# A two-layer language-model tower on one core: how the tables that name each tile's expert are packed, read into registers and placed in TensorE's stream

## The chip, the core and the metric

The kernel runs on one core of a Trainium2 chip. The metric is the device time of one execution in microseconds (us): 1137.43 as the median of three runs, which lie between 1136.9 and 1138.49. Beside the timed runs there is one profiled execution, from which all rows below come.

An engine has two parts that matter here. Its **sequencer** takes the instructions in program order; semaphore waits that stand alone, register arithmetic and register loads are carried out there. Products, copies and activations are handed on to a queue in front of the engine proper, so that a sequencer may be ahead of its engine.

## The reference, cut to what matters

Tokens are embedded and normalised, pass a state-space layer, then a first mixture of experts, then an attention layer, then a second mixture of experts. Only the two mixtures are touched:

```python
# first: 8 experts, 2 picked for each of 4000 tokens, hidden width 512
# second: 64 experts (8 groups of 8), 4 picked for each token, hidden width 256
h = jax.nn.relu(xf @ W1e + b1e)
y = h @ W2e + b2e
acc + cwe[:, None] * y
```

Everything is float32, the width of a token is 128.

## The kernel before

The picked (token, expert) pairs are sorted by expert into blocks of 128 rows. Because an expert's last rows and the next expert's first rows can share a block, the work is cut into **tiles**: one tile is one block under one expert. The first mixture has 63 blocks and 70 tiles, the second 126 blocks and 252 tiles. Which block and which expert a tile has is known only at run time: VectorE writes it into two small int32 tables on one partition, `tile_tables` (for each tile the offset of the expert's second weights, and the place of the next tile's block in the ring of turned blocks) and `stage_tables` (the offset of the expert's first weights).

Each engine's loop over tiles is written out flat; the order in the program is the order of the code, and semaphores tie the engines together. For tile u:

- GpSimd (POOL, line 867) gathers the 128 rows of a block from memory, eight blocks ahead at most.
- TensorE (PE) turns a block (`turn`, line 633), makes the first product of tile u+1 (`first`, line 638), waits for the middle layer of tile u (line 674), and makes its second product (`second`, line 645). Each float32 product of 128 by 128 is carried out as two passes; a tile of the first mixture has 8 + 8 passes, of the second 4 + 4, and a turn is one pass.
- VectorE (DVE) copies a turned block out (line 554), makes half of the bias and relu (`rectify`, line 559) and copies the expert's first weights for tile u+3 into a ring (`stage`, line 550). In the second mixture it later also combines results (line 1328). ScalarE makes the other half of the relu (line 605) and copies results out (line 623).

PE and DVE hold the table's words in registers. The class `Words` keeps 16 registers for a round of eight tiles, four words (two tiles) to a load; after each odd tile the four registers just used are loaded anew for the next round:

```python
self.engine.reg_load(self.regs[2 * u:2 * u + 4], self.table[0:1, bass.ds((first_tile + (self.first + u)) * 2, 4)])
...
second(words.value(u, 0), u)
if u % 2 and first_tile + u + RING < c.tiles:
    words.load(first_tile + RING, u - 1)
```

A word is a finished offset, so `value` needs one fused register instruction, which also forms the address. The second product needs one more for each further 128 rows of the weights.

Of the kernel before, what the change touches and what calls it, by code (L numbers as in the profile page):

```python
# [18 lines left out]
I32 = mybir.dt.int32  # L19
I16 = mybir.dt.int16  # L20
U32 = mybir.dt.uint32
ALU = mybir.AluOpType
ACT = mybir.ActivationFunctionType
AX = mybir.AxisListType

D = 128
# [66 lines left out]
SPAN = 16384  # L93
KEEP = {0: 32, 1: 67}


# [61 lines left out]
def tower_kernel(nc, a, out):  # L158
# [15 lines left out]
    with ExitStack() as ctx:  # L174
# [86 lines left out]
        b1r = sb("b1r", [128, 2, 128])  # L261
        table = sb("table", [1, 2 * TAB], I32)
        w0 = 2 * FFN[0].tab
        assert 2 * w0 <= 2 * TAB <= 512
        tile_tables = [table[0:1, 0:w0], cst[0:1, 128:128 + 2 * TAB].bitcast(I32)]
        stage_tables = [table[0:1, w0:2 * w0], table[0:1, 0:2 * TAB]]
        place = [sb("place", [128, 4, NT], I32)] * 2
# [190 lines left out]

        def pairs_of(engine, table, tau, n, top_a, top_b):

            _, words = nc.values_load_multi_w_load_instructions(
                table[0:1, bass.ds(tau * 2, 2 * n)], engines=[engine], min_val=0, max_val=max(top_a, top_b),
                skip_runtime_bounds_check_because="the tables hold clipped numbers of experts and places in the ring")

            def within(word, top):
                return nc.s_assert_within(word, 0, top, skip_runtime_bounds_check_because="the tables hold clipped numbers")
            return [within(w, top_a) for w in words[0::2]], [within(w, top_b) for w in words[1::2]]

        class Words:

            def __init__(self, engine, p, table, first, top_a, top_b):
                self.engine, self.table, self.first, self.tops = engine, table, first, (top_a, top_b)
                self.regs = [engine.alloc_register(f"{p}word{n}") for n in range(2 * RING)]
                for u in range(0, RING, 2):
                    self.load(0, u)

            def load(self, first_tile, u):
                self.engine.reg_load(self.regs[2 * u:2 * u + 4], self.table[0:1, bass.ds((first_tile + (self.first + u)) * 2, 4)])

            def value(self, u, which):  # L480
                word = self.engine.snap(self.regs[2 * u + which], min_val=0, max_val=max(self.tops))
                return nc.s_assert_within(word, 0, self.tops[which], skip_runtime_bounds_check_because="the tables hold clipped numbers")

            def free(self):
                for r in self.regs:
                    self.engine.free_register(r)
# [55 lines left out]
        def expert_vector(dve, c, combine_pick):  # L542
# [22 lines left out]
            dve.wait_ge(S(f"w{c.n}_ld"), 16 * weight_loads(c))  # L565
            w1, _ = pairs_of(mybir.EngineType.DVE, stage_tables[c.n], 0, 2, (c.E - 1) * c.wcols, (KEEP[c.n] - 1) * 128)
            words = Words(dve, p, stage_tables[c.n], 2, (c.E - 1) * c.wcols, (KEEP[c.n] - 1) * 128)
# [4 lines left out]
            stage(w1[0], 1)  # L572
            dve.wait_ge(S(p + "turned"), 2)
            v.tensor_copy(ring.blocks[:, 128:256], ps[:, 1, 0:128]).then_inc(S(p + "blocks_in"), 1)
            stage(w1[1], 2)
            dve.wait_ge(S(p + "hid_filled"), 3)
            rectify(0)

            def tiles(first_tile, count):
                for u in range(count):  # L580
                    if first_tile + u in c.turn_at:
                        n = c.turn_at[first_tile + u]
                        dve.wait_ge(S(p + "turned"), n + 1)
                        turn(n)
                    dve.wait_ge(S(p + "hid_filled"), first_tile + (u + 4))
                    rectify(u + 1)
                    stage(words.value(u, 0), u + 3)
                    if u % 2 and first_tile + u + RING < c.tiles:
                        words.load(first_tile + RING, u - 1)
                    n = first_tile + u - COMBINE_AT  # L590
                    if c.n and n >= 0 and n % COMBINE_STEP:
                        combine_pick(n - n // COMBINE_STEP - 1)
# [35 lines left out]
        def expert_tensor(pe, c):  # L628
# [19 lines left out]

            words = Words(pe, p, tile_tables[c.n], 0, (c.E - 1) * c.HC * D, (KEEP[c.n] - 1) * 128)
            pe.sem_inc(S(p + "hid_filled"), 2)  # L650
# [11 lines left out]
            def tiles(first_tile, count):  # L662
                for u in range(count):
# [281 lines left out]
        def _(dve):  # L945
# [45 lines left out]
            def route(c, me, dve):  # L991
# [161 lines left out]

                keep = KEEP[f]
                numbers = tileno[0:1, 0:tab]
                tiles_, stages_ = (t_.rearrange("o (t w) -> o t w", w=2) for t_ in (tile_tables[f], stage_tables[f]))
                if f:
                    me.did(TT(out=block, in0=numbers, in1=one, op=ALU.subtract))
# [3 lines left out]
                else:  # L1162
                    me.did(TT(out=block, in0=numbers, in1=one, op=ALU.subtract))
# [1136 lines left out]
```

## Time and profile before

| | |
|---|---|
| median of the timed runs | 1137.43 us |
| profiled execution, from its first to its last instruction | 1221.9 us |
| TensorE busy with products | 802.4 us, 66% of that span |
| VectorE busy | 778.2 us, 64% |
| first mixture's loop over tiles | about 257.7 to 390.9 us |
| second mixture's loop over tiles | about 793.1 to 1140.7 us |
| register loads | 161 on PE, 163 on DVE |

The profiled execution is 84.5 us longer than the median of the timed runs, so its rows can't be read as if the timed runs were made of them one by one. Register, semaphore and load instructions are shown as a sequencer's own rows (PEldq, DVEq) and are not counted as busy. Where the profile says "issue" an engine waited for nothing that the profile shows.

### The profile page before, as it was taken

The numbers are of one execution on the slowest core, as the hardware profiler recorded it, in microseconds if no ns is written. First come the engines' busy times: TensorE is split into PE (matmuls) and PEld (weight loads), VectorE is DVE, ScalarE is ACT, GpSimd is POOL, SyncE is SP. The second block draws the span as 40 slices with busy tenths as digits, with TensorE's granted clock in tenths as the row PEclk, the third lists the DMA queues.
The fourth block names the chain that finished last, engine by engine and source line by source line (L and its number), as shares of the span: only waits on it lengthen the run. The fifth ranks groups of instructions, "written<-read, shape, count | busy, mean of one in ns | idle before, by whom it ended". The sixth has DMA issues, their size and how long they took to land.

```text
span 1221.9 us, 18019 instructions
## 1 busy us (share of the span) xinstructions
PE 802.4 (66%) x5133; PEld 637.8 (52%) x5133; DVE 778.2 (64%) x2305; ACT 437.9 (36%) x1233; POOL 510.6 (42%) x528
## 2 busy tenths in 40 slices
PE   0218963879998248778587511287887897888343
PEld 0105552679998124434255401177776787777332
DVE  7885467656665248888766699855555555666642
ACT  2543241524444134443103304533343444444200
POOL 7841001255540634662101002466664435555574
PEclk9759965579999556666665555599999998999755
DMA  2290089012221287566400404133332223333222
GB/s 69 76 403 37 1 249 309 1 50 70 71 66 38 60 143 140 118 143 131 77 1 1 132 0 127 33 85 85 89 83 81 83 77 87 88 96 94 59 72 75
DMA packets 116599, 112.95 MB, mean 92 GB/s; under 512 B 16403, under 2 KB 102994, under 8 KB 116258
## 3 DMA queue, kind: packets, MB, share of 16 engines
q1 hardware_dynamic: 103228, 84.68, 25.3%
q0 software_dynamic: 13280, 27.13, 8.2%
q8 instruction: 49, 0.80, 0.3%
q14 instruction: 42, 0.34, 0.1%
HBM read 76.15 MB, written 35.57 MB: 91 GB/s over the span
## 4 chain that ended last, share of the span: by engine, by line
PE 55%; DVE 22%; issue 9%; POOL 5%; ACT 4%; DMA 3%; another core or an unknown queue 1%; SPq 0%; DVEq 0%; POOLq 0%; ACTq 0%
PE ps L638 18%; PE ps L645 15%; DVE wide L1348 6%; PE ps L1969 4%; POOL wide L810 3%; PE ps L633 3%; DVE wide L1229 3%; PE ps L2231 3%; PE ps L2139 2%; PE ps L2180 2%; ACT wide L1757 2%; DVE bnst L955 2%; POOL wide L874 1%; PE ps L2076 1%; PE ps L2224 1%
## 5 line engine op out<-in xcount | busy, mean ns | idle before, releaser
L645 PE MATMUL ps<-big,wide 128*128 x1568 | 238.1, 282 | 33.9 <-ACT wide L605 20.6
L638 PE MATMUL ps<-wide 128*128 (+1 forms) x1580 | 247.1, 287 | 18.9 <-DVE wide L554 12.2
L867 POOL DMA_INDIRECT wide<-xrows,holder x189 | 182.8, 967 | 158.1 <-PE ps L633 116.1
L559 DVE TENSOR_SCALAR wide<-ps,wide 128x128 f32<-128x128 f32 x395 | 131.7, 348 | 156.9 <-PE ps L638 138.4
L638 PEld LDWEIGHTS ps<-wide 128*128 128x128 f32 x1580 | 206.2, 195 | 40.8 <-issue 32.9
L645 PEld LDWEIGHTS ps<-big,wide 128*128 128x128 f32 x1568 | 203.7, 194 | 44.5 <-issue 43.9
L605 ACT ACTIVATE wide<-ps,wide 128x128 f32<-128x128 f32 x395 | 137.8, 367 | 202.4 <-PE ps L638 184.9
L1348 DVE TENSOR_REDUCE wide<-ps 125x3 f32<-125x1500 f32 (+1 forms) x96 | 143.7, 1540 | 46.7 <-PE ps L1969 45.3
L874 POOL DMA_INDIRECT wide<-results,place x128 | 127.6, 997 | 100.1 <-DVE h L1328 44.0
L1969 PE MATMUL ps<-big 97*125 97x500 bf16 x256 | 104.8, 545 | 40.3 <-DVE wide L1348 32.5
L623 ACT COPY wide<-ps 128x128 f32<-128x128 f32 x322 | 85.2, 264 | 92.1 <-PE ps L645 78.1
L550 DVE COPY wide<-big 128x258 f32 (+2 forms) x328 | 107.4, 327 | 3.9 <-issue 3.8
L856 POOL TENSOR_SCALAR wide<-tileno,sm 125x128 f16<-125x128 f16 x36 | 23.5, 653 | 172.2 <-DVE sm L1210 143.0
L1969 PEld LDWEIGHTS ps<-big 97*125 97x125 bf16 x256 | 42.6, 191 | 89.5 <-DVE wide L1348 50.8
L901 POOL DMA_INDIRECT wide<-results,place x64 | 60.9, 952 | 60.4 <-SPq L540 34.3
L554 DVE COPY wide<-ps 128x128 f32<-128x128 f32 x185 | 53.7, 290 | 41.5 <-PE ps L633 33.5
L1328 DVE SCALAR_TENSOR_TENSOR h<-wide,gate,h 125x128 f32<-125x128 f32 x128 | 43.2, 350 | 28.7 <-DMA wide<-results,place 23.4
L2248 PE MATMUL ps<-wide 125*128 125x79 f16 (+2 forms) x192 | 22.1, 262 | 54.6 <-DVE wide L1229 49.7
L633 PE MATMUL ps<-cst,wide 128*128 128x128 f32 x189 | 53.7, 287 | 5.5 <-issue 5.2
L1757 ACT ACTIVATE wide<-h,shift,rs 125x128 f32<-125x128 f32 x112 | 45.2, 483 | 25.6 <-DVE shift L972 19.4
L2119 PE MATMUL ps<-cst,wide 125*128 125x125 f32 x96 | 20.9, 370 | 48.6 <-ACT wide L1757 48.4
L2231 PE MATMUL ps<-b,cst 8*125 8x128 f32 (+1 forms) x128 | 33.0, 435 | 24.8 <-issue 20.6
(388 smaller groups left out, 1102.7 us busy)
## 6 DMA issues: line engine op xcount, KB each, us to landing
results<-wide SPq DMA_DIRECT2D x161, 128.0 KB, 1.8
big<-kappa SPq DMA_DIRECT2D x8, 1750.0 KB, 21.0
big<-parts SPq DMA_DIRECT2D x96, 125.0 KB
big<-in_L_ffn_W_dram SPq DMA_DIRECT2D x10, 1024.0 KB, 9.4
big<-in_L_ffn_W_dram SPq DMA_DIRECT2D x64, 128.0 KB, 2.6
parts<-wide SPq DMA_DIRECT2D x24, 250.0 KB
xrows<-wide SPq DMA_DIRECT2D x2, 1792.0 KB
wide<-results,place POOLq DMA_INDIRECT x192
```

The costliest lines, as they stand in the source:

```text
L550: v.tensor_copy(ring.w1[u % U], w1v[:, bass.ds(w1, c.wcols)]).then_inc(S(p + "w1_ready"), 1)
L559: last = v.tensor_scalar(ring.hid[u % 2][:, 128 * k:128 * k + 128], ps[:, 4 + u % 2, 128 * k:128 * k + 128], w[:, hid + k:hid + k + 1], 0. ...
L605: last = s.activation(ring.hid[u % 2][:, 128 * k:128 * k + 128], ps[:, 2 + u % 2, 128 * k:128 * k + 128], ACT.Relu, bias=w[:, hid + k:hid ...
L623: s.copy(ring.res[u], ps[:, 6 + u % 2, 0:D]).then_inc(S(p + "res_ready"), 1)
L633: t.transpose(ps[:, u % 2, 0:128], ring.rows[u % RING], ident).then_inc(S(p + "turned"), 1)
L638: last = t.matmul(ps[:, (2 if k < c.HC // 2 else 4) + u % 2, 128 * k:128 * k + 128], ring.w1[u % U][:, 128 * k:128 * k + 128], turned, sta ...
L645: last = t.matmul(ps[:, 6 + u % 2, 0:D], ring.hid[u % 2][:, 128 * k:128 * k + 128], w[:, D * k:D * k + D], start=k == 0, stop=k == c.HC - 1)
L867: gp.indirect_dma_start(ring.rows[j % RING], None, xrows[:, :], bass.IndirectOffsetOnAxis(ap=holder[:, j:j + 1], axis=0)).then_inc(S(f"row ...
L874: gp.indirect_dma_start(ring.rows[n % 8], None, results[1 if n < FIRST_PICKS else 2][:, :], bass.IndirectOffsetOnAxis(ap=place[f][:, k, t: ...
L1348: v.tensor_reduce(out=mcol[:, j, H * b + lo:H * b + hi], in_=ps[0:R, 3 * (n % 2):3 * (n % 2) + hi - lo, 0:L], axis=AX.X, op=ALU.max).then_ ...
L1969: last = t.matmul(ps[0:R, 3 * (n % 2) + head - lo, 0:L], stack[0:SROWS, 0, b % 2, head, R * j:R * j + R], stack[0:SROWS, 1, b % 2, head, : ...
L2231: last = t.matmul(p[0:R, D * j:D * j + D], cT[0:c.E, R * j:R * j + R], b2[0:c.E, f, :], start=True, stop=True)
```

## The change

The tables become bytes. A tile has the number of its expert in one byte and, for PE, the number of its block's place in the ring in the next; DVE's table has the expert's number alone. `Words` reads the bytes as 32-bit words: a load brings a whole round of eight tiles, four words on PE and two on DVE, into one of two sets of registers. What was an offset is now taken out of its word by a shift, a mask and a product with the length of one entry. Loads come once in eight tiles: on PE between the first product and the wait for the middle layer at the fourth tile of a round, on DVE ahead of the copy of weights at the third.

```diff
-                reg_load(self.regs[2 * u:2 * u + 4], self.table[0:1, bass.ds((first_tile + (self.first + u)) * 2, 4)])
+            def load(self, turn):
+                at_ = turn * self.count
+                self.engine.reg_load(self.sets[turn % 2], self.table[0:1, at_:at_ + self.count])
...
+            def value(self, tile, byte, scale, top):
+                per = 4 * self.count // RING
+                word, bit = divmod(8 * (tile % RING * per + byte), 32)
+                reg = self.engine.snap(self.sets[tile // RING % 2][word])
+                field = (reg >> bit if bit else reg) & 255
+                return nc.s_assert_within(field * scale, 0, top * scale, ...)
...
-                    stage(words.value(u, 0), u + 3)
-                    if u % 2 and first_tile + u + RING < c.tiles:
-                        words.load(first_tile + RING, u - 1)
+                    if u == DVE_WORDS_AT and first_tile + RING < c.tiles:
+                        words.load(first_tile // RING + 1)
+                        stage(words.value(first_tile + u + 3, 0, c.wcols, c.E - 1), u + 3)
...
-                    first(u + 1, words.value(u, 1))
+                    first(u + 1, words.value(first_tile + u + 1, 1, 128, KEEP[c.n] - 1))
+                    if u == PE_WORDS_AT and first_tile + RING < c.tiles:
+                        words.load(first_tile // RING + 1)
                     pe.wait_ge(S(p + "hid_dve"), first_tile + (u + 3))
                     pe.wait_ge(S(p + "hid_act"), first_tile + (u + 3))
-                    second(words.value(u, 0), u)
-                    if u % 2 and first_tile + u + RING < c.tiles:
-                        words.load(first_tile + RING, u - 1)
+                    second(words.value(first_tile + u, 0, c.HC * D, c.E - 1), u)
...
-                me.did(TS(tiles_[:, :, 0], one, float(c.HC * D), None, ALU.mult))
-                me.did(TS(stages_[:, 0:tab - 1, 0], one[:, 1:tab], float(c.wcols), None, ALU.mult))
-                me.then(TS(wrap, numbers, float(keep), -128.0 * keep, ALU.is_ge, ALU.mult))
-                me.did(v.scalar_tensor_tensor(stages_[:, :, 1], numbers, 128.0, wrap, ALU.mult, ALU.add))
+                me.did(v.tensor_copy(tiles_[:, :, 0], one))
+                me.did(v.tensor_copy(stage_tables[f], one))
                 me.settle()
-                me.then(TS(wrap, block, float(keep), -128.0 * keep, ALU.is_ge, ALU.mult))
-                me.then(v.scalar_tensor_tensor(tiles_[:, 0:tab - 1, 1], block[:, 1:tab], 128.0, wrap[:, 1:tab], ALU.mult, ALU.add))
+                me.then(TS(wrap, block, keep, -keep, ALU.is_ge, ALU.mult))
+                me.then(TT(out=tiles_[:, :, 1], in0=block, in1=wrap, op=ALU.add))
```

PE's stream in the second mixture before, from the first product of one tile to the first product of the next, after an odd tile. "ISA" is a fused register instruction, TENSOR_LOAD a register load, and the words in brackets are the semaphores that an instruction waits for: `f1_hid_act` and `f1_hid_dve` the middle layer, `f1_w1_ready` the copied weights, `f1_blocks_in` the turned block.

```order
L638 MATMUL ps<-wide 128x128 x2
L481 ISA [waits f1_hid_act,f1_hid_dve]
L645 MATMUL ps<-big,wide 128x128
L645 ISA
L645 MATMUL ps<-big,wide 128x128
L478 TENSOR_LOAD cst
L633 MATMUL ps<-cst,wide 128x128 [waits f1_blocks_in,row_ld4]
L481 ISA [waits f1_w1_ready,f1_blocks_in]
L638 MATMUL ps<-wide 128x128 x2
```

The same place now, after the fourth tile of a round, where the load of the next round stands.

```order
L637 MATMUL ps<-wide 128x128 x2
L471 TENSOR_LOAD table
L476 ISA [waits f1_hid_act,f1_hid_dve]
L644 REGISTER_ALU
L644 ISA
L644 MATMUL ps<-big,wide 128x128
L644 ISA
L644 MATMUL ps<-big,wide 128x128
L632 MATMUL ps<-cst,wide 128x128 [waits f1_blocks_in,row_ld6]
L476 ISA [waits f1_w1_ready,f1_blocks_in]
```

The load has moved from behind the second product to before the wait for the middle layer, and is gone from three of four pairs of tiles; behind each of the two waits two register instructions have come in (the last `ISA` shown is followed by another `REGISTER_ALU` and another `ISA` before the next first product). Where a field lies lowest in its word, the first of the three is a plain move, which these rows leave out. PE has 161 loads before and 41 now, 1106 fused register instructions before and 1589 now, with 644 register operations and 161 moves that were not there.

DVE's stream at the start of the second mixture's loop before, from the holder of block numbers to the first copies; the first `TENSOR_LOAD` belongs to a helper that is gone now.

```order
L1217 TENSOR_SCALAR holder<-ps 128x47 [waits bank_filled]
L461 TENSOR_LOAD table [waits emptied_dve,w1_ld]
L478 TENSOR_LOAD table x4
L550 COPY wide<-big 128x258 [waits bank_filled]
L571 COPY wide<-ps 128x128 [waits f1_turned]
L550 ISA
L550 COPY wide<-big 128x258
```

And DVE's stream in the loop now, one tile and the beginning of the next, with the load at the third tile.

```order
L555 TENSOR_SCALAR wide<-ps,wide 128x128 [waits f1_hid_filled]
L546 REGISTER_ALU
L546 ISA
L546 COPY wide<-big 128x258
L550 COPY wide<-ps 128x128 [waits f1_turned]
L555 TENSOR_SCALAR wide<-ps,wide 128x128 [waits f1_hid_filled]
L471 TENSOR_LOAD table
L476 ISA
L546 REGISTER_ALU
L546 ISA
```

At the start DVE's five loads become one. In the loop a copy of weights stood behind one `ISA` and now stands behind three register instructions.

## Rows read from the trace of the kernel before

**Rows 1.** The page: span, and the chain that ended last by engine.
```profile
span 1221.9 us, 18019 instructions
...
PE 55%; DVE 22%; issue 9%; POOL 5%; ACT 4%; DMA 3%; another core or an unknown queue 1%; SPq 0%; DVEq 0%; POOLq 0%; ACTq 0%
```
**Rows 2.** Stretches of the second mixture; passes of line 638 in brackets.
```profile
core 0: us, PE busy (x) PEld busy (x), PEclk, DMA share, GB/s
793.10:910.70 117.60, 53.91 (x309) 42.52 (x309) 0.96 0.30 85
910.70:998.60 87.90, 42.91 (x261) 34.07 (x262) 1.00 0.28 80
998.60:1140.70 142.10, 72.79 (x441) 58.56 (x442) 0.98 0.31 89
...
```
**Rows 3.** Register loads of line 478: count, ns least/median/most, first and last start.
```profile
L478 PEldq TENSOR_LOAD <-cst x126: 327/333/616, 790.4 to 1132.6; - x126
...
L478 PEldq TENSOR_LOAD <-cst x4: 327/328/333, 790.4 to 791.6; - x4
```
**Rows 4.** Register instructions of line 481: second mixture, one plain tile, one with turn.
```profile
L481 PEldq FUSED_REGOPS  x504: 49/53/59, 793.6 to 1140.9; - x168
...
L481 PEldq FUSED_REGOPS  x3: 49/49/53, 1098.0 to 1098.6; - x3
...
L481 PEldq FUSED_REGOPS  x3: 49/49/53, 901.0 to 901.8; - x3
```
**Rows 5.** PE in order of time, second mixture, tiles without a turn.
```profile
1098.08 0.71 PE L638 MATMUL ps<-wide 128*128 x4 [0.15 <-issue]
...
1099.07 0.61 PE L638 MATMUL ps<-wide 128*128 x4
1099.51 0.64 PE L645 MATMUL ps<-big,wide 128*128 x4
1100.20 0.71 PE L638 MATMUL ps<-wide 128*128 x4
```
**Rows 6.** PE's weight loads, second mixture, a turn and the first product behind it.
```profile
900.86 0.14 PEld L633 LDWEIGHTS ps<-cst,wide 128*128 128x128 f32 x1
901.12 0.52 PEld L638 LDWEIGHTS ps<-wide 128*128 128x128 f32 x4
```
**Rows 7.** PE in order of time, second mixture, tiles with a turn.
```profile
862.06 0.71 PE L638 MATMUL ps<-wide 128*128 x4 [0.34 <-DVE wide L554]
...
863.16 0.61 PE L638 MATMUL ps<-wide 128*128 x4
...
864.39 0.71 PE L638 MATMUL ps<-wide 128*128 x4
```
**Rows 8.** All engines in order of time, second mixture: ScalarE after a pause.
```profile
903.39 0.27 ACT L623 COPY wide<-ps 128x128 f32<-128x128 f32 x1 [1.12 <-PE ps L645]
```
**Rows 9.** The same view, first mixture: first products of two tiles.
```profile
300.87 1.06 PE L638 MATMUL ps<-wide 128*128 x8
...
302.76 1.06 PE L638 MATMUL ps<-wide 128*128 x8
```
**Rows 10.** The same view: POOL's gather, DVE's rectify and copy of weights.
```profile
901.90 0.35 DVE L559 TENSOR_SCALAR wide<-ps,wide 128x128 f32<-128x128 f32 x1 [0.34 <-PE ps L638]
...
902.17 0.28 DVE L550 COPY wide<-big 128x258 f32 x1
902.38 0.94 POOL L867 DMA_INDIRECT wide<-xrows,holder  x1 [0.30 <-issue]
```
**Rows 11.** The same view: the start of the first mixture's loop.
```profile
254.14 0.67 DVE L1306 TENSOR_SCALAR big<-ps 1x500 bf16<-1x500 f32 x1 [1.92 <-PE ps L1938]
256.51 0.43 DVE L550 COPY wide<-big 128x516 f32<-128x516 f32 x1 [1.71 <-issue]
```
**Rows 12.** DVE in order of time: the tables of the first mixture.
```profile
201.34 0.18 DVE L1164 TENSOR_SCALAR table<-wide 1x80 int32<-1x80 f32 x1
...
202.53 0.42 DVE L1174 TENSOR_TENSOR wide<-wide 125x256 f32<-125x256 f32 x1
```

More of the change, by code:

```diff
@@ L21 @@
 U32 = mybir.dt.uint32
+U8 = mybir.dt.uint8
 ALU = mybir.AluOpType
@@ L94 @@
 KEEP = {0: 32, 1: 67}
+PE_WORDS_AT = 3
+DVE_WORDS_AT = 2
 def ap(t, offset, dims):
@@ L261, in tower_kernel @@
         b1r = sb("b1r", [128, 2, 128])
-        table = sb("table", [1, 2 * TAB], I32)
+        table = sb("table", [1, 4 * TAB], U8)
         w0 = 2 * FFN[0].tab
-        assert 2 * w0 <= 2 * TAB <= 512
-        tile_tables = [table[0:1, 0:w0], cst[0:1, 128:128 + 2 * TAB].bitcast(I32)]
-        stage_tables = [table[0:1, w0:2 * w0], table[0:1, 0:2 * TAB]]
+        assert w0 % 16 == 0 and w0 + FFN[0].tab <= TAB
+        tile_tables = [table[0:1, 0:w0], table[0:1, TAB:3 * TAB]]
+        stage_tables = [table[0:1, w0:w0 + FFN[0].tab], table[0:1, 3 * TAB:4 * TAB]]
         place = [sb("place", [128, 4, NT], I32)] * 2
@@ L457, in weight_loads @@
             return c.E // (8 if c.n else 4) + (W2_EARLY if c.n else 8)
[L459 to L467, printed above, removed]
@@ L469, in tower_kernel, with __init__ @@
-        class Words:
[L471 to L482, printed above, removed]
+        class Words:
+            def __init__(self, engine, p, table, tiles):
+                self.engine, self.table, self.tiles = engine, table.bitcast(I32), tiles
+                self.count = table.shape[-1] * RING // (4 * tiles)
+                self.sets = [[engine.alloc_register(f"{p}word{k}_{n}") for n in range(self.count)] for k in range(2)]
+            def load(self, turn):
[6 more added lines that the diff above has]
+                field = (reg >> bit if bit else reg) & 255
+                return nc.s_assert_within(field * scale, 0, top * scale, skip_runtime_bounds_check_because="the tables hold clipped numbers")
@@ L484, in free @@
             def free(self):
-                for r in self.regs:
+                for r in self.sets[0] + self.sets[1]:
                     self.engine.free_register(r)
@@ L565, in expert_vector @@
             dve.wait_ge(S(f"w{c.n}_ld"), 16 * weight_loads(c))
-            w1, _ = pairs_of(mybir.EngineType.DVE, stage_tables[c.n], 0, 2, (c.E - 1) * c.wcols, (KEEP[c.n] - 1) * 128)
-            words = Words(dve, p, stage_tables[c.n], 2, (c.E - 1) * c.wcols, (KEEP[c.n] - 1) * 128)
+            words = Words(dve, p, stage_tables[c.n], c.tab)
+            words.load(0)
             dve.wait_ge(S("bank_filled"), nfill[at[f"holder{c.n}", len(c.parts) - 1]])
@@ L571, in expert_vector @@
             v.tensor_copy(ring.blocks[:, 0:128], ps[:, 0, 0:128]).then_inc(S(p + "blocks_in"), 1)
-            stage(w1[0], 1)
+            stage(words.value(1, 0, c.wcols, c.E - 1), 1)
             dve.wait_ge(S(p + "turned"), 2)
             v.tensor_copy(ring.blocks[:, 128:256], ps[:, 1, 0:128]).then_inc(S(p + "blocks_in"), 1)
-            stage(w1[1], 2)
+            stage(words.value(2, 0, c.wcols, c.E - 1), 2)
             dve.wait_ge(S(p + "hid_filled"), 3)
@@ L586, in tiles @@
                     rectify(u + 1)
-                    stage(words.value(u, 0), u + 3)
-                    if u % 2 and first_tile + u + RING < c.tiles:
-                        words.load(first_tile + RING, u - 1)
+                    if u == DVE_WORDS_AT and first_tile + RING < c.tiles:
+                        words.load(first_tile // RING + 1)
+                    if first_tile + u + 3 < c.tiles:
+                        stage(words.value(first_tile + u + 3, 0, c.wcols, c.E - 1), u + 3)
+                    else:
+                        stage(0, u + 3)
                     n = first_tile + u - COMBINE_AT
@@ L647, in second @@
                 last.then_inc(S(p + "res_filled"), 1)
-            words = Words(pe, p, tile_tables[c.n], 0, (c.E - 1) * c.HC * D, (KEEP[c.n] - 1) * 128)
+            words = Words(pe, p, tile_tables[c.n], c.tab)
+            words.load(0)
             pe.sem_inc(S(p + "hid_filled"), 2)
@@ L1152, in route @@
                 dve.wait_ge(S("emptied_dve"), nth[at[f"expert{f}", 0]])
-                keep = KEEP[f]
+                keep = float(KEEP[f])
                 numbers = tileno[0:1, 0:tab]
-                tiles_, stages_ = (t_.rearrange("o (t w) -> o t w", w=2) for t_ in (tile_tables[f], stage_tables[f]))
+                tiles_ = tile_tables[f].rearrange("o (t w) -> o t w", w=2)
+                me.did(TT(out=block, in0=numbers, in1=one, op=ALU.subtract))
                 if f:
-                    me.did(TT(out=block, in0=numbers, in1=one, op=ALU.subtract))
                     me.then(TS(second, one, float(c.E), None, ALU.is_ge))
```

2 lines of the change are left out of this document (removed).

## The prediction

> **What bounds the kernel now.** I read the page first [rows 1]: the chain that ended last is PE for 55% and "issue" for 9% of a span of 1221.9 us. Then the second mixture by stretches [rows 2]: 793.1 to 1140.7 us, 347.6 us for 252 tiles, at a granted clock of 0.96 to 1.00, which is the upper of the two levels. Four passes make a first product, so the stretches hold 77, 65 and 110 tiles. In the code the first has a turn in each tile, the second in three of four, the third in none. Here PE is not at its own pace. A pass takes 0.111 us (below, from the first mixture), so a plain tile with its eight needs 0.89; but the first products of three tiles start at 1098.08, 1099.07 and 1100.20 [rows 5], 0.99 and 1.13 apart, 2.12 for the pair, 1.06 for a tile. With a turn the engine's own work is nine passes, 1.00, and the pair in [rows 7] takes 1.10 and 1.23, 2.33; pairs beside it are shorter, and I use 1.12 for a tile.
>
> Who holds PE up? Its sequencer. One plain tile's instructions go by from 1098.0 to 1098.6 [rows 4], 0.6 us, and one with a turn from 901.0 to 901.8, 0.75 when the tenths are allowed for. A load comes once in two tiles: four in a row start at 790.4 to 791.6, 0.40 us from one to the next [rows 3], of which the row itself is 0.33. So the pair costs the sequencer 1.6 us against 1.78 for the engine: less, but the sequencer can't run far ahead, because it must wait in each tile for the middle layer. From that wait the second product, the load, the next wait and the first product of the tile after that follow in a row; ScalarE and VectorE then answer, and the wait of two tiles later ends. This round of two tiles takes the 2.12 us, and its load is 0.40 of them. The first mixture has the same loads, but sixteen passes to hide them: its tiles come 1.89 apart [rows 9], 17 passes of 0.111, so PE itself is the bound there.
>
> Beside this there are pauses, such as one of 1.12 us ahead of a copy on ScalarE [rows 8], whose product PE had done by then. Undisturbed the second mixture would take 77 x 1.12 + 65 x 1.10 + 110 x 1.06 = 274 us, 73 us less than its 347.6. The profiled span is 84.5 us above the median of the timed runs. I take the pauses to belong to the profiled execution, make the sum with undisturbed tiles and add it to 1137.43.
>
> **The change part by part.** *Loads out of the loop.* 120 of 161 go on PE. One load is worth 0.40 in the round of two tiles.
>
> *Register instructions into the loop.* For each field there were one instruction and now three: four more for each tile, all on the sequencer, two behind each wait. The trace shows no lone mask and no move. The nearest rows are the fused instructions: their own rows are 0.05 us [rows 4], the low end. The high end comes from [rows 6]: between the weight load of a turn and that of the next first product lie one semaphore and one fused instruction and 0.26 us, 0.13 each with the handing on of products. A plain tile has six such instructions and hands on four products in 0.6, so 0.10 each at most. I take 0.10 and keep 0.05 and 0.13.
> The trace's 0.05 is the time of carrying out alone. The Trainium skill says so in Perfetto Trace Analysis, section Per-instruction lifecycle: the profiled window of a sequencer-only instruction leaves out fetch, decode and the wait. This speaks against the change, since by the row alone the four new ones would cost 0.2 for a tile and with what lies around them 0.4; the 0.26 of the rows agrees with the rule.
>
> *The second mixture, plain tiles (110).* Sequencer 0.6 + 4 x 0.10 = 1.00, and one load in eight tiles 0.05: 1.05. The round of two tiles: 2.12 - 0.40 + 4 x 0.10 = 2.12, and now for every tile, not the odd ones alone. So 1.06, and the load of each round, which stands just before a wait that the sequencer reaches only some 0.1 us early, adds 0.3/8 = 0.04 where the other round doesn't take it up; I take half. 1.08 against 1.06: +2.2 us.
> *Tiles with a turn (77).* 0.75 + 0.40 + 0.05 = 1.20 against 1.12. But POOL's gather takes 0.94 + 0.30 = 1.24 [rows 10] and each tile needs one; eight blocks of lead make 77 x 1.24 - 8 x 1.12 = 86.5, 1.12 a tile, so part of the 0.08 is there already whenever the lead has run out. I take 0.03 x 77 = +2.5.
> *The 65 between.* 0.75 x 1.20 + 0.25 x 1.08 = 1.17 against 1.10: +4.5. POOL has more time here, 1.24 for 1.33 tiles.
> Together +9.2. With 0.05 for an instruction the round is 1.92 and the sequencer 0.85, so 0.98 for a plain tile; -9 for these, -5 for the middle ones, none for the first, where POOL holds: -14. With 0.13 the sequencer needs 1.17, 1.32 and 1.28: +11, +15, +12, together +38, less what POOL takes, some +30.
>
> *DVE's loop.* Two more instructions between rectify and the copy of weights, which follow each other 0.27 apart now [rows 10]: some 0.36 then. DVE idles 0.34 in that tile, and its copy is for a tile two further on: nothing. If that cover went, 0.1 a tile would show.
> *The first mixture's loop.* Sequencer about 1.3 + 0.4 against 1.89 of passes: nothing. In eight rounds the load may show, at most 8 x 0.1.
> *The starts.* DVE's copy of weights waits for five loads, 254.14 + 0.67 to 256.51 [rows 11]; PE's four of 0.40 run beside them. One of each stays: 3 x 0.40 = 1.2 us for each mixture, -2.4; DVE's new instructions there are 0.2 and take it to -2.2.
> *The tables.* From 201.34 to 202.53, 1.19 us for the first mixture [rows 12], on DVE with nobody else at work. Six operations become four, and the loss is that of the third and fourth: an estimate of 0.4 there and, with 256 columns instead of 80, of 0.7 in the second mixture; -1.1.
> *Register words.* The Trainium skill gives a floor of some 0.6 us for a register load (DMA: Bandwidth & Descriptors, section Latency and other measured facts). By that a load would be worth 0.2 more in each round than I have it, and the change would gain some 20 us more; the 0.40 of [rows 3] is measured in place, and I keep it.
>
> Sum: +9.2 - 2.2 - 1.1 = +5.9, 1143.3; I say **1143**.
>
> **The rivals.** *Cheap instructions.* A mask or move costs little more than its row, as the 0.05 suggests; the round falls to 1.92 and PE nears its own 0.89. -14 - 3.3, about 1121; with half of that 1128. For it: every shown register row is 0.05. Against it: the 0.6 us for a tile.
> *The sequencer is no bound where nothing is recorded.* If recording also lengthens each instruction, the timed runs are held by POOL's 1.24 and by PE's passes, and both the loads and the new instructions lie in slack. Then only starts and tables are left: 1134. For it: the difference of 84.5 is 11 more than the pauses explain. Against it: 0.99 and 1.13 alternate just as the loads do. This one ends not slower.
> *Dear instructions.* 0.13 and more behind each wait: 1137.4 + 30 - 3.3 = 1164, and with half the excess 1153.
> *Loads that don't hide.* The load ahead of the wait shows whole, 31 x 0.4 = 12 us in the second mixture. Counted so far are 2.2 in the plain tiles and about 65 x 0.75 x 0.05 = 2.4 in the middle ones, so 1143 + 8 = 1151.
>
> **How the numbers follow.** A measurement of this kernel can tell about 0.2%, 2.3 us, from no change. Forecast, 1139 to 1148: 0.40. Cheap: 0.17, all of it faster. No bound: 0.27, of this faster 0.07, same 0.18, slower 0.02. Dear: 0.09; loads that show: 0.07; both slower. Of the forecast 0.05 is within 0.2%. Faster 0.24, same 0.23, slower 0.53. The range leaves out the far halves of the cheap and the dear case: 1128 to 1155.
>
> **What the changed profile would show.** In plain tiles of the second mixture the first products evenly 1.05 to 1.10 apart instead of 0.99 and 1.13, with one longer in eight; PE's "issue" waits before both products instead of before line 638 alone; register rows of about 0.05 whose starts are 0.10 apart. The first mixture stays at 1.89. The start at 254.14 gets 1.2 us shorter. I am wrong if plain tiles come below 1.0 undisturbed, or if a lone mask takes 0.13 and more from start to start.

## The result, and the profile after

The changed kernel takes 1157.97 us (median; 1156.47 to 1161.14) against 1137.16 for the kernel before, measured beside it: 1.019 times the time, with a 95% interval of 1.016 to 1.022. It is slower by 20.8 us; 5.8 were forecast, and the range ended at 1155.

The page of the changed kernel, its span and the chain of waits, the lines that answer to [rows 1]:

```profile
span 1159.4 us, 19697 instructions
...
PE 56%; DVE 26%; POOL 5%; DMA 4%; ACT 4%; issue 4%; SPq 0%; DVEq 0%; ACTq 0%; POOLq 0%
```

This profiled execution is as long as the timed runs, while that of [rows 1] was 84.5 us longer than its own. So the two profiles can't be subtracted from each other as they stand. The kernel before was therefore profiled once more (first experiment). Its second profile has a span of 1136.2, and the stretches of the second mixture below stand for [rows 2] from here on. First product only; the columns are the stretch and its length, PE's busy time with passes in brackets, the same for weight loads, the granted clock, the DMA share and GB/s. The kernel before:

```profile
780.50:874.20 93.70, 53.11 (x308) 42.88 (x308) 0.95 0.39 105
874.20:946.10 71.90, 42.86 (x261) 34.13 (x262) 1.00 0.37 101
946.10:1061.70 115.60, 72.11 (x440) 57.62 (x441) 1.00 0.41 110
```

The changed kernel, the same stretches of 77 tiles with a turn, 65 with three turns in four, 110 without:

```profile
779.60:877.90 98.30, 55.46 (x309) 41.52 (x309) 0.97 0.38 102
877.90:958.30 80.40, 45.91 (x261) 33.85 (x261) 1.00 0.32 88
958.30:1085.40 127.10, 77.72 (x440) 57.34 (x441) 1.00 0.37 100
```

The loop went from 281.2 to 305.8 us: +4.6, +8.5 and +11.5. The clock is the same to 0.02. All else together is 1.4 us shorter than in the other profile. So the loss lies in the second mixture's loop, and the largest part of it in the plain tiles, where 2.2 were forecast.

Plain tiles in order of time, PE (start, length, operation, passes), changed kernel; this answers to [rows 5]:

```profile
1073.97 0.71 PE L637 MATMUL ps<-wide 128*128 x4
...
1075.24 0.71 PE L637 MATMUL ps<-wide 128*128 x4
...
1076.30 0.71 PE L637 MATMUL ps<-wide 128*128 x4
1077.36 0.71 PE L644 MATMUL ps<-big,wide 128*128 x4 [0.36 <-issue]
1077.93 0.71 PE L637 MATMUL ps<-wide 128*128 x4
```

The first products come 1.27, 1.06 and 1.63 us apart. The last is the tile with the load. Over the third stretch the median of a tile is 1.09, and every eighth takes 1.41 to 1.70, mostly 1.65. The alternation of 0.99 and 1.13 is gone, and PE's 0.36 ahead of the second product is put down to "issue". What its sequencer did in that tile, by lines (count, ns, first and last start; the window is this tile, but that of line 676 runs on, with this tile's wait and then without it):

```profile
L637 PEldq FUSED_REGOPS  x1: 46/46/46, 1076.2 to 1076.2; - x1
L471 PEldq TENSOR_LOAD <-table x1: 549/549/549, 1076.3 to 1076.3; - x1
...
L676 PEldq EVENT_SEMAPHORE  x6: 51/51/51, 1076.9 to 1082.3; - x6
L676 PEldq EVENT_SEMAPHORE  x5: 51/51/51, 1078.0 to 1082.3; - x5
```

And the two engines that make the middle layer. TensorE waits for VectorE's half in line 675 and for ScalarE's in line 676:

```profile
1075.98 0.37 ACT L604 ACTIVATE wide<-ps,wide 128x128 f32<-128x128 f32 x1 [0.40 <-PE ps L637]
...
1077.04 0.37 ACT L604 ACTIVATE wide<-ps,wide 128x128 f32<-128x128 f32 x1 [0.35 <-PE ps L637]
...
1077.37 0.34 DVE L555 TENSOR_SCALAR wide<-ps,wide 128x128 f32<-128x128 f32 x1
...
1081.92 0.37 ACT L604 ACTIVATE wide<-ps,wide 128x128 f32<-128x128 f32 x1 [0.35 <-PE ps L637]
```

These rows hold the main result. The middle layer for the wait at 1076.9 was done at 1075.98 + 0.37 = 1076.35, as the load began. The one for the wait at 1078.0 was done by ScalarE at 1077.41 and by VectorE at 1077.37 + 0.34 = 1077.71, still 0.3 us before the sequencer came to ask. So in the tile with the load and in the next one no other engine keeps TensorE waiting: the load's 0.55 stands in its sequencer's way, and both waits come late.

The other tiles are different. From 1078.0 to 1082.3 four more go by, 1.08 us each, and the last of these waits ends just as ScalarE does, at 1081.92 + 0.37 = 1082.29. In the trace's own times, which are finer than the rows print, 66 of the 110 waits of line 676 in the third stretch end less than 0.045 us after ScalarE's half, nearly all of them 0.036 or 0.037 after it; 26 of the other 44 belong to a tile with a load or to the next one. The 66 still hang on the answer of ScalarE, in the round of two tiles that the prediction describes. The sequencer is not far from being the bound there too. From the last register instruction ahead of the wait to the wait's end it takes 0.124 us at the least and 0.167 in the median, so it comes some 0.04 early at most; in the tiles right behind a load, whose middle layer is long done, the same step is 0.15 to 0.28.

The rows of the loads, for the whole run, which answer to [rows 3]:

```profile
L471 PEldq TENSOR_LOAD <-table x41: 332/522/621, 256.9 to 1076.3; - x41
L471 DVEq TENSOR_LOAD <-table x41: 522/539/817, 256.5 to 1076.0; - x41
```

One load on PE takes 0.52 in the median instead of 0.33, VectorE's two words take 0.54.

### The profile page after: what moved, and what is told of

Same layout as the page of the kernel before. It is cut to its first block, busy times and chain, and to the rows that moved or that the text cites. A ratio compares the mean times of both kernels' runs of the same rounds, so it can differ in the third digit from the quotient of the medians.

```text
span 1159.4 us, 19697 instructions
## 1 busy us (share of the span) xinstructions
PE 804.3 (69%) x5133; PEld 642.7 (55%) x5133; DVE 785.1 (68%) x2301; ACT 447.4 (39%) x1233; POOL 508.6 (44%) x528
## 4 chain that ended last, share of the span: by engine, by line
PE 56%; DVE 26%; POOL 5%; DMA 4%; ACT 4%; issue 4%; SPq 0%; DVEq 0%; ACTq 0%; POOLq 0%
PE ps L637 19%; PE ps L644 17%; DVE wide L1344 7%; PE ps L1965 4%; POOL wide L874 3%; DVE wide L1225 3%; PE ps L2135 2%; PE ps L2176 2%; ACT wide L1753 2%; PE ps L632 2%; DVE bnst L955 2%; PE ps L2227 1%; DMA wide<-results,place 1%; POOL wide L810 1%; PE ps L1956 1%
## 5 line engine op out<-in xcount | busy, mean ns | idle before, releaser
L637 PE MATMUL ps<-wide 128*128 (+1 forms) x1580 | 256.5, 293 | 0.7 <-DVE wide L567 0.5
L644 PEld LDWEIGHTS ps<-big,wide 128*128 128x128 f32 x1568 | 201.0, 192 | 18.6 <-issue 16.9
L546 DVE COPY wide<-big 128x258 f32 (+2 forms) x328 | 112.6, 343 | 25.1 <-issue 24.0
L1225 DVE TENSOR_SCALAR wide<-tileno,sm,tokno 125x79 f16<-125x79 f16 (+2 forms) x192 | 47.0, 317 | 1.7
```

Source lines behind the costliest of these rows:

```text
L546: v.tensor_copy(ring.w1[u % U], w1v[:, bass.ds(w1, c.wcols)]).then_inc(S(p + "w1_ready"), 1)
L637: last = t.matmul(ps[:, (2 if k < c.HC // 2 else 4) + u % 2, 128 * k:128 * k + 128], ring.w1[u % U][:, 128 * k:128 * k + 128], turned, sta ...
L644: last = t.matmul(ps[:, 6 + u % 2, 0:D], ring.hid[u % 2][:, 128 * k:128 * k + 128], w[:, D * k:D * k + D], start=k == 0, stop=k == c.HC - 1)
L1225: last = TS(hot_tile[:, g % 2, j, 0:hi - lo], tileno[0:R, lo:hi], sm[:, 4 + k, t:t + 1], tokno[:, t:t + 1], ALU.is_equal, ALU.mult)
```

## The experiments

**The kernel before, once more.**

> The kernel before, unchanged, for a second profile of it. The first one was 84.5 us longer than the timed runs; the profile of the changed kernel (span 1159.4) is not. Outside the second mixture's loop the changed kernel can have gained at most the 3.3 us of starts and tables, and its loop takes 305.8 us, so in the timed runs the loop before must take about 305.8 - 20.8 - 3.3 = 282 us. Theory (the pauses belong to that one execution): if this profile is an undisturbed one, its second mixture takes 280 to 285 us, with pairs of plain tiles of 2.1 to 2.2 us. Rival (the pauses are in every execution and the changed kernel has lost them): 340 us again, and the time that the changed kernel gave back is lost elsewhere.

Measured: 1137.94 us, and a profile of 1136.2 with the three stretches shown above, 281.2 us. Plain tiles, PE:

```profile
1041.45 0.61 PE L638 MATMUL ps<-wide 128*128 x4
...
1042.58 0.71 PE L638 MATMUL ps<-wide 128*128 x4
...
1043.57 0.61 PE L638 MATMUL ps<-wide 128*128 x4
```

1.13 and 0.99 again, 2.12 for the pair. The pauses belonged to the first profiled execution, and its undisturbed tiles had been read rightly: the plain stretch worked out at 116.6 is 115.6.

**The arithmetic alone.** The loads stay as they were, a mask without effect brings four register instructions to a tile.

```diff
                 word = self.engine.snap(self.regs[2 * u + which], ...)
+                if self.masked:
+                    word = word & 0xfffff
```

> The kernel before, its finished offsets and its 161 loads where they were, but each field on TensorE passes through a move and a mask without effect: four more register instructions for a tile, as many as the change adds, and nothing else of the change. Theory (the change is a trade: register instructions for loads, both on a sequencer that is the bound): from the changed kernel's loop of 305.8 us, its 31 loads of 0.57 taken off and 122 loads of 0.40 put on, 305.8 - 18 + 49 = 337 us against 281 before, +56 us, 1193; the first mixture stays at 1.90. So the loads that the change took out would be worth 1193 - 1158 - 3 = 32 us and the instructions that it brought cost 56. Rival (the loads hid before, and hide beside the new instructions too): the same as the changed kernel without its load, 305.8 - 18 = 288, 1144.

Measured: 1178.47 us, 1.035 times the kernel before (1.031 to 1.039). The second mixture's three stretches:

```profile
778.20:881.10 102.90, 55.29 (x308) 41.69 (x308) 0.97 0.36 98
881.10:964.60 83.50, 45.69 (x260) 33.88 (x260) 1.00 0.31 84
964.60:1099.50 134.90, 76.86 (x440) 57.34 (x440) 1.00 0.35 94
```

321.3 us, 40 more than before, not 56. The rival is out. The theory's size is too large because it put a load's full step of 0.40 on every pair of the changed kernel's tiles: here tiles of 0.99 and 1.46 alternate (first products at 1079.85, 1080.84 and 1082.30), 2.45 for a pair. That is about the old round of 2.12 and four instructions of 0.09. So the change is a trade: the instructions that it brings are worth 40 us with the old loads beside them, and going from these loads to the few new ones, at their new place, gives back 321.3 - 305.8 = 15.5.

**The price of a register instruction.** One more mask for each field of the changed kernel.

```diff
                 field = (reg >> bit if bit else reg) & 255
+                for _ in range(self.more):
+                    field = self.engine.snap(field) & 255
```

> The changed kernel with one more mask (& 255, without effect) for each field on TensorE: two more register instructions for a tile, one behind each wait, 140 in the first mixture and 504 in the second. Theory (the sequencer is the bound in all of the second mixture, a mask steps by 0.093 us in its trace, and the first mixture hides it): 504 x 0.093 = +47 us, 1205, plain tiles 1.28 instead of 1.09, and the first mixture at 1.90 as before. Rival (only part of the register instructions is on the path, and the loss of the change was in its load): +10 to +20 us, 1168 to 1178.

Measured: 1196.84 us, 1.053 (1.049 to 1.057), 38.9 above the changed kernel; the loop takes 344.2, 38.4 more:

```profile
773.20:883.90 110.70, 55.30 (x308) 41.34 (x308) 0.98 0.33 91
883.90:974.30 90.40, 45.94 (x260) 33.88 (x260) 1.00 0.28 78
974.30:1117.40 143.10, 77.73 (x440) 57.33 (x440) 1.00 0.33 89
...
L639 PEldq ALU_OP  x644: 32/32/42, 257.3 to 1117.2; - x161
```

504 masks for 38.4 us, 0.076 each, though their own rows show 0.032. From one mask's start to the next instruction's it is 0.093, as the theory has it. Part of that is hidden: the masks first use up the 0.04 by which the sequencer came early, and PE's load became shorter at the same time (0.34 instead of 0.52 in the median). Here the sequencer is the bound in every plain tile: of the 110 waits for the middle layer in the third stretch none ends less than 0.1 us after ScalarE's half, where 66 ended less than 0.045 after it in the changed kernel. The first mixture stayed at 1.90 for a tile.

**The load's place.** The changed kernel, its load moved behind the second product of the same tile.

```diff
-                    if u == PE_WORDS_AT and first_tile + RING < c.tiles:
-                        words.load(first_tile // RING + 1)
                     pe.wait_ge(S(p + "hid_dve"), first_tile + (u + 3))
                     pe.wait_ge(S(p + "hid_act"), first_tile + (u + 3))
                     second(words.value(first_tile + u, 0, c.HC * D, c.E - 1), u)
+                    if u == PE_WORDS_AT and first_tile + RING < c.tiles:
+                        words.load(first_tile // RING + 1)
```

> The changed kernel with TensorE's load behind the second product of the fourth tile instead of before the wait for the middle layer; nothing else. Theory (sequencer bound everywhere): the place hardly matters, only the load's own row may be shorter there, 0.33 to 0.43 instead of 0.55 as before; 31 x 0.1 to 0.2 = 3 to 6 us less, 1152 to 1155, and the tiles with a load still stand out by 0.4. Rival (the place is at fault: behind the second product the load would lie beside four passes already handed on): 12 to 18 us less, 1140 to 1146. Second rival (place worth nothing): 1158.

Measured: 1156.3 us, 1.013 (1.008 to 1.018) times the kernel before, an interval that overlaps the changed kernel's. The profiles tell more: the loop takes 300.2, 5.6 less than in the changed kernel. PE's load and the tile that holds it:

```profile
L471 PEldq TENSOR_LOAD <-table x41: 327/332/517, 257.0 to 1073.0; - x41
...
1063.24 0.71 PE L637 MATMUL ps<-wide 128*128 x4
...
1064.65 0.71 PE L637 MATMUL ps<-wide 128*128 x4 [0.25 <-issue]
```

The load is 0.33 here and its tile 1.41. The rows and the loop agree with the theory; the timed runs alone, just above its 1152 to 1155, can't tell it from the second rival. So some 0.2 us of each load go with its place in this tile, where its row is that much longer, and 0.35 show at either place.

**A second load.** The words of a round are loaded again at its first tile.

```diff
                     if u == PE_WORDS_AT and first_tile + RING < c.tiles:
                         words.load(first_tile // RING + 1)
+                    if u == 0 and first_tile:
+                        words.load(first_tile // RING)
```

> The changed kernel with a second load for each round: at the first tile of a round, ahead of the wait for the middle layer, TensorE loads the round's four words again into the set that holds them already (31 more loads in the second mixture, 8 in the first). Theory (with three register instructions for a field TensorE's sequencer has no slack left in the second mixture, so that a load shows with its whole row and its step, 0.33 to 0.55 and 0.08): 31 x 0.41 to 0.63 = 13 to 20 us more, 1171 to 1178; the first tile of a round comes to stand out by as much as the fourth, and the first mixture stays at 1.90. Rival (the 0.57 at the fourth tile comes from something else that falls in this tile, such as VectorE's load one tile earlier): 0 to 5 us more, 1158 to 1163, and the first tile of a round stays near 1.1.

Measured: 1168.87 us, 1.029 (1.026 to 1.033), 10.9 above the changed kernel, between the theory's 1171 and the rival's 1163; the loop takes 315.4, 9.6 more. That is 0.31 for each of 31 loads, below the theory's 0.41 and far above the rival's 0.16. The new tile stands out by 0.3 to 0.45, and the old one by a little less than before. A new load and the old one of the same round:

```profile
L471 PEldq TENSOR_LOAD <-table x1: 332/332/332, 1060.3 to 1060.3; - x1
...
L471 PEldq TENSOR_LOAD <-table x1: 447/447/447, 1063.9 to 1063.9; - x1
```

Both stand between a first product and the wait for the middle layer. The new load's row is 0.33 in all 31 rounds, the old one's 0.39 to 0.60 in 29 of 31, so this place alone doesn't make a load long. A load shows almost whole wherever it stands in this loop. TensorE without any load has not been measured: with words of other tiles the places in the ring no longer fit the semaphores.

**One load of 16 words.** The kernel before, finished offsets, one load for a round.

```diff
-                    if u % 2 and first_tile + u + RING < c.tiles:
-                        words.load(first_tile + RING, u - 1)
+                    if u == 3 and first_tile + RING < c.tiles:
+                        words.load(first_tile // RING + 1)
```

> The kernel before with its finished offsets, but TensorE loads the 16 words of a whole round at once, into one of two sets of registers, behind the second product of the fourth tile; no register arithmetic is added, and VectorE, the tables and the starts stay but for TensorE's one load instead of four. Theory: the sequencer needs about 0.69 us for a plain tile and 0.05 to 0.07 for its part of the load, less than the 0.89 of TensorE's passes, so that the passes become the bound: (1.06 - 0.92) x 110 + (1.10 - 1.03) x 65 and little in the first 77 tiles, which POOL's gather holds at about 1.12: 15 + 5 + 1 = 21 us less than before, 1116. Rival (a load of 16 words takes four times as long as one of four): about before, 1137. Rival (the timed runs of before are not held by the sequencer at all): 1137 as well, but with a short load row.

Measured: 1140.24 us, 1.003 (1.001 to 1.005): no gain, a shade slower. The load's row, and PE around one:

```profile
L496 PEldq TENSOR_LOAD <-cst x32: 1102/1139/1247, 776.2 to 1054.4; - x32
...
1052.90 0.61 PE L656 MATMUL ps<-wide 128*128 x4
...
1053.80 0.61 PE L656 MATMUL ps<-wide 128*128 x4
...
1055.80 0.71 PE L656 MATMUL ps<-wide 128*128 x4 [0.92 <-DVE wide L568]
...
1056.79 0.61 PE L656 MATMUL ps<-wide 128*128 x4
```

The first rival is right: sixteen words take 1.1 us, where four loads of four words have 1.32 between them. Of eight plain tiles seven now come 0.89 to 1.02 apart, PE's own pace, and the eighth takes 2.0. The profile puts that idle 0.92 down to VectorE's copy of weights, the semaphore that came last; with the load at 1054.4 and 1.12 long, PE's sequencer could not ask before 1055.5. So a round loses about as much to one long load as it did to four short ones. And the half of the theory that concerns the tiles without a load is shown: with finished offsets, and no load in the way, TensorE's passes are the bound.

**The words in smaller loads.** Two words behind every tile instead of four behind every odd one.

```diff
-                    if u % 2 and first_tile + u + RING < c.tiles:
-                        words.load(first_tile + RING, u - 1)
+                    if first_tile + u + RING < c.tiles:
+                        words.load_one(first_tile + RING, u)
```

> The kernel before, with TensorE's load of four words behind every odd tile cut into loads of two words behind every tile: twice as many loads, the same words. The runs so far give 0.33 us for four words and 1.11 for sixteen, about 0.065 for a word and 0.07 for a load. Theory (the price goes by words, and the load stands in a round of two tiles: of an odd and the next odd, or an even and the next even): each round now holds a load of 0.20 instead of none or 0.33; rounds of 1.99 instead of 2.12, both kinds alike, (2.12 - 1.99) / 2 x 252 = 16 us less at most, 1121 to 1130. Rival (the price goes by loads, 0.33 each): 2.12 stays or grows, 1137 to 1150.

Measured: 1182.31 us, 1.040 (1.036 to 1.043). Both the theory and the rival fall, and the row says why:

```profile
L481 PEldq TENSOR_LOAD <-cst x244: 530/536/717, 784.1 to 1099.0; - x122
```

A load of two words takes 0.54, more than one of four (0.33). 244 of them instead of 126 loads of 0.33 are the loss: the loop takes 324.3.

**The load's place without the arithmetic.** The kernel before with its loads of four words, but between the first product and the wait for the middle layer.

```diff
                     first(u + 1, words.value(u, 1))
+                    ahead = first_tile + u + 5
+                    if u % 2 and RING <= ahead < c.tiles:
+                        words.load(ahead - ahead % RING, ahead % RING)
                     pe.wait_ge(S(p + "hid_dve"), first_tile + (u + 3))
                     pe.wait_ge(S(p + "hid_act"), first_tile + (u + 3))
                     second(words.value(u, 0), u)
-                    if u % 2 and first_tile + u + RING < c.tiles:
-                        words.load(first_tile + RING, u - 1)
```

> The kernel before with finished offsets and loads of four words, but each load stands between the first product and the wait for the middle layer (where the changed kernel has its load), and brings the words of the two tiles that come five and six later. No register arithmetic is added. Theory (a load delays the end of a round of two tiles only when the sequencer would otherwise go on; between the first product and the wait it idles, as the profile of the kernel that loads 16 words at once shows in its tiles without a load, 0.89 to 0.92 long): most of the 0.30 a pair goes, plain tiles come at 0.92 to 0.98 instead of 1.06, tiles with a turn at 1.02 to 1.08; 110 x 0.10 + 142 x 0.05 = 18 us less, 1119. Rival (the place is bad in itself: there the row is 0.55 instead of 0.33, as in the changed kernel): the pair stays at 2.1 or grows, 1137 to 1160.

Measured: **1119.13 us**, 0.985 times the kernel before (0.981 to 0.989), faster than both kernels. The stretches and a load with its tile:

```profile
778.00:870.30 92.30, 49.80 (x308) 41.32 (x308) 0.98 0.39 106
870.30:936.60 66.30, 40.04 (x260) 34.22 (x261) 1.00 0.40 110
936.60:1040.10 103.50, 67.19 (x440) 57.87 (x441) 1.00 0.45 121
...
L478 PEldq TENSOR_LOAD <-cst x1: 335/335/335, 1028.9 to 1028.9; - x1
...
1028.10 0.61 PE L638 MATMUL ps<-wide 128*128 x4
...
1029.00 0.61 PE L638 MATMUL ps<-wide 128*128 x4
...
1030.06 0.61 PE L638 MATMUL ps<-wide 128*128 x4
```

262.1 us for the loop, 19.1 less, and 0.94 for a plain tile. ScalarE's half of the middle layer runs from 1028.75 to 1029.12, the load from 1028.9 to 1029.24. The load fills time in which the sequencer would have waited, and the tile behind it grows from 0.89 to 1.09 at most in this stretch. So the place that the change chose is good. The same place did not help the changed kernel, whose sequencer comes some 0.04 early at most.

**VectorE's load.** Two variants of the changed kernel: in the first, VectorE's load stands at the first tile of a round; in the second, it brings four words for sixteen tiles.

```diff
-DVE_WORDS_AT = 2
+DVE_WORDS_AT = 0
```

> The changed kernel with VectorE's load at the first tile of a round instead of the third, so that the loads of VectorE and TensorE no longer run at the same time. In the changed kernel TensorE's load takes 0.55 us in most rounds of the second mixture, 0.33 with the load behind the second product. Theory A (the two loads disturb each other): 0.33 here too. Theory B (it is the place behind the first product): 0.45 to 0.62 as before. The time: 1152 under A, 1158 under B.

```diff
-            words = Words(dve, p, stage_tables[c.n], c.tab)
+            words = Words(dve, p, stage_tables[c.n], c.tab, 2 * RING)
```

> The changed kernel, but VectorE loads four words for sixteen tiles instead of two words for eight: 20 loads instead of 41, at the third tile of every second round. TensorE is as in the changed kernel. In the changed kernel VectorE's load of two words takes 0.525 us at least; TensorE's loads of two words took 0.54 in the kernel with two words for every tile, those of four words 0.33. Theory (VectorE's loads are off the path, and TensorE's load is what makes one tile in eight 0.57 longer): 1155 to 1159, the tiles with a load at 1.6 as before in every round. Rival (VectorE's loads hold up the middle layer, or lengthen TensorE's load row beside them): in every second round the tile is shorter by 0.2, 16 x 0.2 = 3 us, and a load of 0.34 instead of 0.53 in the others another 2; 1150 to 1154.

Measured: 1168.5 us in a single run for the first, above both of its theories; 1161.65 for the second, above its range but at 1.019 (1.015 to 1.024) times the kernel before, which is the changed kernel's own ratio. The loads of the second:

```profile
L472 PEldq TENSOR_LOAD <-table x41: 330/529/617, 257.1 to 1075.1; - x41
L472 DVEq TENSOR_LOAD <-table x21: 340/344/611, 256.6 to 1056.1; - x21
```

VectorE's load fell from 0.54 to 0.34 and is gone from every second round, and nothing followed: the loop takes 305.9, PE's load 0.53, whether VectorE has a load in that round or not. At the third tile VectorE's load is off the path. It is not so everywhere: at the first tile it made the loop 310.1, with PE waiting 0.44 for the copy of weights in a tile. There PE's load was 0.38 in the median, between the two theories. What makes PE's load last 0.55 in the changed kernel, and 0.33 in the median at the same place in the kernel of 1119 us and at the first tile of a round in the kernel with two loads, stays open; that the two engines' loads run side by side is not what it takes.

## Why the prediction was wrong

**What bounds the kernel.** Right. The loop waited on TensorE's sequencer and a round of two tiles of 2.12; the second profile has the same pair, and 281.2 us against the 274 worked out. Most of the 7 lies in the first stretch (93.7 against 86), in a few long tiles at its start and end. The pauses belonged to one execution; the rival that the sequencer holds nothing up in the timed runs is dead, since both the arithmetic and the loads move them.

**The price of a register instruction.** Right enough: 0.10 was taken, 0.093 from start to start and 0.076 net are measured for a mask. The row alone (0.032) would have been far off.

**The starts and the tables.** Right. The start of the first mixture on VectorE, as in [rows 11], in the second profile of the kernel before and then in the changed kernel:

```profile
256.92 0.67 DVE L1306 TENSOR_SCALAR big<-ps 1x500 bf16<-1x500 f32 x1 [1.92 <-PE ps L1938]
259.29 0.43 DVE L550 COPY wide<-big 128x516 f32<-128x516 f32 x1 [1.70 <-issue]
```

```profile
256.24 0.67 DVE L1302 TENSOR_SCALAR big<-ps 1x500 bf16<-1x500 f32 x1 [1.92 <-PE ps L1934]
257.28 0.43 DVE L546 COPY wide<-big 128x516 f32<-128x516 f32 x1 [0.38 <-issue]
```

From the first to the copy of weights there were 2.37 us, now 1.04; what is left of that at the first rectify is 1.1 us in each mixture, 2.2 together, as forecast. The tables take 0.38 and 0.64 less for the forecast 0.4 and 0.7.

**VectorE's loop and the first mixture.** Right, both nothing; the first mixture's tiles are 1.90 in every run but that with 16 words in a load.

**The loads that stay.** Here it failed. "... the load of each round, which stands just before a wait that the sequencer reaches only some 0.1 us early, adds 0.3/8 = 0.04 where the other round doesn't take it up; I take half." The load adds 0.57 to its tile, and hardly anything takes it up. Three things were wrong. The load's row is 0.52 there, and from its start to the wait behind it 0.63 go by in the plain stretch, where 0.40 was taken; the trace of before could not show that duration for this place. The sequencer comes some 0.04 early at most, not 0.1. And the half that the other round was to take up had no reason behind it: one sequencer goes through both rounds in turn, so a late wait makes the next one late too, as the rows of 1076.9 and 1078.0 show, and the tile behind gives back 0.05 (1.04 instead of 1.09). A sum that spreads the load over eight tiles, 0.05 for each, hides this: the little time to spare in a tile can't be saved up for the eighth. Over the second mixture these are 31 x 0.57 = 17.7 us by the tiles of the profile, where some 4.6 were counted: 13 of the 15 us that the forecast lacks. A run puts the price of a further load at 0.31, the one with the load moved at 0.35 for a load of 0.33; the rest is the long row.

**The sequencer's own sum.** Right. The 0.6 us read from the three starts of [rows 4] is one full period, from one first product's register instruction to the next one's. In the changed kernel the median steps of a plain tile's instructions, with 0.124 for the step to the wait, add up to 1.0, as forecast; the tiles right behind a load, which wait for nothing, take 1.07 from wait to wait. The tiles without a load take 1.09 in the median instead of the forecast 1.06 with its 0.02, most of them in the round of two tiles. So the bound of these tiles was right, but sum and round lie so close that a load has nowhere to hide.

So the rival "loads that don't hide" was the case, at the 7% it was given, and dearer than its 0.40 for a load: 1151 was its time, 1157.97 was measured.

| term, us | forecast | measured |
|---|---|---|
| second mixture, 77 tiles with a turn | +2.5 | +4.6 |
| 65 with three turns in four | +4.5 | +8.5 |
| 110 plain tiles | +2.2 | +11.5 |
| starts | -2.2 | -2.2 |
| tables | -1.1 | -1.0 |
| sum | +5.9 | +21.4; timed +20.8 |

## What to carry to other kernels

A load of registers is hidden only where the sequencer would have waited anyway, and only for as long as it would have waited in that very tile: time to spare in the other tiles doesn't add up for it. Add up the sequencer's instructions over one full period, compare the sum with what sets the period, and charge what the load has beyond the difference in full. Fewer loads bought with more register arithmetic is a bad trade for an engine whose sequencer is near its limit: here 40 us of arithmetic against 15 of loads. The gain that was there lay in the place alone, 18 us for a few lines, with the table's finished offsets kept.

## What the runs showed of the hardware

A load's time does not simply follow its words: on TensorE 0.33 us for four words (up to 0.62 at the changed kernel's place), 1.1 for sixteen, but 0.54 for two; on VectorE 0.34 for four and 0.52 at least for two. The Trainium skill gives one floor of some 0.6 us for a register load (DMA: Bandwidth & Descriptors, section Latency and other measured facts). The rows here disagree for four words and come near it for two.

A mask shows a row of 0.032 us and takes the sequencer 0.093 from its start to the next instruction's.
